# Experts' phase of an adaLN block with fast weights and mixture of experts: inner columns split 128 + 48, short down products of two tiles in the halves of the array

## What is computed

```python
B, S, D, E, F, FS = (4, 256, 256, 64, 176, 352)   # weights: w_gate, w_up (E, F, D), w_down (E, D, F)
...
buf = jnp.zeros((E, C, D), x.dtype).at[se, pos_c].add(jnp.where(valid[:, None], x[st], jnp.zeros((), x.dtype)))
g = jnp.einsum('ecd,efd->ecf', buf, w_gate)
u = jnp.einsum('ecd,efd->ecf', buf, w_up)
eo = jnp.einsum('ecf,edf->ecd', jax.nn.silu(g) * u, w_down)
```

## Time and profile before

| | us |
|---|---|
| median of 3 runs | 2373.19 (2371.55 to 2373.62) |
| profiled execution, its own time | 2371.46 |
| its span | 2369.4 |
| experts' phase in it (first gather issued to last copy-out) | about 1411.8 to 2060.5 |
| combine, behind it | to the end |

### The profile page before, as it was taken

The page is one execution under the profiler, slowest core; times in us unless marked ns, Lnnn a source line. Parts: engine busy times, 40 slices in busy tenths (PEclk is TensorE's granted clock), DMA queues, the critical chain, the costliest instruction groups (busy, mean ns, idle before and its releaser), DMA issues. The chain is left out here.

```text
span 2369.4 us, 41529 instructions
## 1 busy us (share of the span) xinstructions
PE 1772.2 (75%) x11445; PEld 1300.8 (55%) x11514; DVE 1265.8 (53%) x3323; ACT 939.5 (40%) x2156; POOL 899.2 (38%) x836
## 2 busy tenths in 40 slices
PE   3667638999999999846610539999999999875663
PEld 1444426777777777634500117777777777654542
DVE  2444426888888888635459972222222222245554
ACT  1232225777777777511101843333333333321110
POOL 1222312333333333345505014344433444257776
PEclk7666757999999999856655989999999999987776
DMA  2333341111111111045510016665556545444544
GB/s 69 101 113 97 93 125 24 42 42 42 42 42 42 42 42 42 23 116 145 148 40 0 1 33 180 185 180 170 166 166 171 170 134 105 107 119 140 149 136 124
DMA packets 269891, 231.43 MB, mean 98 GB/s; under 512 B 88624, under 2 KB 246672, under 8 KB 269728
## 3 DMA queue, kind: packets, MB, share of 16 engines
q1 hardware_dynamic: 211360, 136.99, 20.9%
q0 software_dynamic: 21504, 58.75, 9.9%
q10 hardware_dynamic: 36864, 33.57, 4.3%
HBM read 156.56 MB, written 72.65 MB: 97 GB/s over the span
## 5 line engine op out<-in xcount | busy, mean ns | idle before, releaser
L1698 POOL DMA_INDIRECT e_xg<-scratch_h,slots x256 | 255.6, 999 | 369.9 <-PE e_psX L1712 359.4
L1809 DVE COPY e_hT<-e_psH 88x256 f32<-88x256 f32 x256 | 107.7, 421 | 467.9 <-PE e_psH L1735 467.9
L1726 PE MATMUL e_psGU<-e_wgu,e_xT 128*128 x1024 | 349.5, 463 | 1.7 <-issue 0.9
L1742 PE MATMUL e_psD<-e_wd,e_hT 88*128 x1024 | 263.6, 379 | 0.0
L1075 POOL TENSOR_TENSOR f_wnr<-f_wss,f_half 128x4 f32<-128x4 f32 x96 | 111.1, 1157 | 390.5 <-DVE f_wss L1023 390.5
L1726 PEld LDWEIGHTS e_psGU<-e_wgu,e_xT 128*128 128x128 f32 x1024 | 192.0, 191 | 76.3 <-issue 6.9
L1930 POOL DMA_INDIRECT c_g<-scratch_eo,c_idx x192 | 196.3, 1023 | 76.0 <-issue 46.0
L1742 PEld LDWEIGHTS e_psD<-e_wd,e_hT 88*128 88x128 f32 x1024 | 173.8, 190 | 14.3 <-issue 0.3
L1787 ACT ACTIVATE e_eo<-e_psD 128x256 f32<-128x256 f32 x256 | 98.3, 384 | 179.2 <-PE e_psD L1742 179.2
L1777 ACT ACTIVATE e_sgm<-e_psGU 128x176 f32<-128x176 f32 x256 | 81.3, 318 | 212.3 <-PE e_psGU L1726 212.3
L354 PE MATMUL q_psQ<-q_wqkv,q_hT 128*128 128x512 f32 (+1 forms) x256 | 125.6, 649 | 31.6 <-DVE q_zl L430 29.8
(11 more groups left out here) (287 smaller groups left out, 4301.1 us busy)
## 6 DMA issues: line engine op xcount, KB each, us to landing
scratch_eo<-e_eo ACTq DMA_DIRECT2D x256, 128.0 KB, 1.8
scratch_qkvT<-q_tT SPq DMA_DIRECT2D x32, 384.0 KB, 2.8
e_wgu<-in_wgT SPq DMA_DIRECT2D x64, 176.0 KB
e_wgu<-in_wuT SPq DMA_DIRECT2D x64, 176.0 KB
e_wd<-in_wdT SPq DMA_DIRECT2D x64, 176.0 KB
scratch_kv<-q_y SPq DMA_DIRECT2D x32, 256.0 KB, 2.2
f_kvT<-scratch_qkvT SPq DMA_DIRECT2D x128, 64.0 KB
f_kv<-scratch_kv SPq DMA_DIRECT2D x64, 128.0 KB
```

Of the source, the lines that this page charges most:

```text
L1698: pool.indirect_dma_start(out=xg[n % GB][:, :], out_offset=None, in_=T["h2"], in_offset=bass.IndirectOffsetOnAxis(slots[:, n:n + 1], 0), b ...
L1726: mm = pe.matmul(psGU[:, j % 2, 0:2 * F], xT[:, j % 2, k, :], wgu[:, bass.ds(buf, 1), k, :].rearrange("p b n -> p (b n)"), start=(k == 0), ...
L1742: mm = pe.matmul(psD[:, j % 2, 0:D], hT[0:FH, j % 2, k, :], wd[0:FH, buf, k, :].rearrange("p b n -> p (b n)"), start=(k == 0), stop=(k == 1))
L1809: v.tensor_copy(hT[0:FH, b, :, :].rearrange("p k t -> p (k t)"), psH[0:FH, b, 0:2 * P]).then_inc(htd, 1)
```

## The change

The 176 inner columns are cut as 128 + 48 instead of 88 + 88.

- `hh` gets 64 columns of zeros between the two pieces. An even tile's short piece stands right behind its 128 columns, an odd tile's 64 columns further. The second transpose turns 48 columns for an even tile and 112 (the zeros and its own 48) for an odd one. So the 48 rows of the short piece come to stand at partition 0 or at partition 64.
- SyncE loads the down weights in three DMAs instead of one: 128 rows, and the last 48 rows twice, at partitions 0 and 64.
- VectorE copies the 48 rows of the tile's expert to a new buffer `wt`, for which it reads the expert from `need` and waits for `ready`. It makes two copies of `hT` (128 rows, 48 rows) instead of one and two products `hh` (128 columns, 48 columns) instead of one. `hT` is four tiles deep instead of two.
- TensorE does `down` for two tiles at once, in the step in which the odd one is due: the 128-row products of both, then the 48-row products of both, the even tile's on the partitions from 0, the odd tile's on those from 64. In the other step there is no `down`.

ScalarE's, POOL's and the other phases' programs are not touched.

```diff
@@ SyncE
-                sp.dma_start(wd[0:FH, bass.ds(buf, 1), :, :].rearrange("p b k n -> p (b k) n"), ...
-                sp.wait_ge(w_in, (ex + 1) * 48)
+                for rows, part, lo in ((P, 0, 0), (FT, 0, P), (FT, HP, P)):
+                    sp.dma_start(wd[part:part + rows, bass.ds(buf, 1), lo // P, :].rearrange("p b n -> p (b n)"),
+                                 T["wdT"][bass.ds(ex, 1), lo:lo + rows, :].rearrange("e p n -> (e p) n")).then_inc(w_in, 16)
+                sp.wait_ge(w_in, (ex + 1) * 80)
@@ TensorE (FT = 48, HP = 64)
             def turn_h(n, j):
+                part = HP * (n % 2)
                 pe.wait_ge(hd, thru(n))
                 pe.wait_ge(htd, thru(n - 2))
-                pe.transpose(psH[0:FH, j % 2, 0:P], hh[:, j % 2, 0:FH], ident[:, :])
-                pe.transpose(psH[0:FH, j % 2, P:2 * P], hh[:, j % 2, FH:F], ident[:, :]).then_inc(hp, 1)
...
+                pe.transpose(psH[:, j % 2, 0:P], hh[:, j % 2, 0:P], ident[:, :])
+                pe.transpose(psH[0:part + FT, j % 2, P:2 * P], hh[:, j % 2, P:P + part + FT], ident[:, :]).then_inc(hp, 1)
+
+            def down(n, experts):
+                for m in (n - 1, n):
+                    pe.wait_ge(htd, thru(m))
+                    pe.wait_ge(eod, thru(m - 2))
+                    pe.matmul(psD[:, m % 2, 0:D], hT[:, m % 4, 0, :],
+                              wd[:, bass.ds(experts[m % 2], 1), 0, :].rearrange("p b n -> p (b n)"), start=True, stop=False)
+                for m in (n - 1, n):
+                    part = HP * (m % 2)
+                    pe.matmul(psD[:, m % 2, 0:D], hT[part:part + FT, m % 4, 1, :], wt[part:part + FT, m // 2 % 2, :],
+                              start=False, stop=True).then_inc(dp, 1)
...
-                if real(n, 3):
-                    down(n - 3, (j - 3) % TI, out_of)
+                if real(n, 3) and (n - 3) % 2 == 1:
+                    down(n - 3, out_of)
@@ VectorE
+            v.memset(hh[:, 1, P:P + HP], 0.0).then_inc(blank, 1)
+            v.wait_ge(blank, 1)
...
                     v.wait_ge(hp, thru(m))
-                    v.wait_ge(dp, thru(m - 2))
-                    v.tensor_copy(hT[0:FH, b, :, :].rearrange("p k t -> p (k t)"), psH[0:FH, b, 0:2 * P]).then_inc(htd, 1)
+                    v.wait_ge(dp, thru(m - 4))
+                    part = HP * (m % 2)
+                    expert = v.value_load(need[0:1, m:m + 1], min_val=1, max_val=E)
+                    buf = bass.ds(v.snap((expert + (NB - 1)) % NB), 1)
+                    v.wait_ge(ready, expert)
+                    v.tensor_copy(wt[part:part + FT, m // 2 % 2, :], wd[part:part + FT, buf, 1, :].rearrange("p b n -> p (b n)"))
+                    v.tensor_copy(hT[:, m % 4, 0, :], psH[:, b, 0:P])
+                    v.tensor_copy(hT[part:part + FT, m % 4, 1, :], psH[part:part + FT, b, P:2 * P]).then_inc(htd, 1)
...
-                    v.tensor_tensor(hh[:, b, :], psGU[:, b, F:2 * F], sgm[:, b, :], ALU.mult).then_inc(hd, 1)
+                    part = P + HP * (n % 2)
+                    v.tensor_tensor(hh[:, b, 0:P], psGU[:, b, F:F + P], sgm[:, b, 0:P], ALU.mult)
+                    v.tensor_tensor(hh[:, b, part:part + FT], psGU[:, b, F + P:2 * F], sgm[:, b, P:F], ALU.mult).then_inc(hd, 1)
```

More of the change, by code:

```diff
@@ L1623, in phase_experts @@
     TI = 8
-    FH = F // 2
+    FT = F - P
+    HP = P // 2
     GB = 8
@@ L1641, in phase_experts @@
         sgm = sb("sgm", [P, 2, F])
-        hh = sb("hh", [P, 2, F])
-        hT = sb("hT", [P, 2, 2, P])
+        hh = sb("hh", [P, 2, P + HP + FT])
+        hT = sb("hT", [P, 4, 2, P])
+        wt = sb("wt", [P, 2, D])
         eo = sb("eo", [P, OB, D])
@@ L1655, in phase_experts @@
             "xp", "x", "gup", "sg", "h", "hp", "ht", "dp", "eo"))
+        blank = sems.take("e_blank")
         block = ctx.enter_context(nc.Block())
@@ L1681, in _ @@
                                  [bass.ds(ex, 1), :, :, :].rearrange("e p k n -> (e p) k n")).then_inc(w_in, 16)
-                sp.dma_start(wd[0:FH, bass.ds(buf, 1), :, :].rearrange("p b k n -> p (b k) n"),
-                             T["wdT"].rearrange("e (k p) n -> e p k n", p=FH)
-                             [bass.ds(ex, 1), :, :, :].rearrange("e p k n -> (e p) k n")).then_inc(w_in, 16)
-                sp.wait_ge(w_in, (ex + 1) * 48)
+                for rows, part, lo in ((P, 0, 0), (FT, 0, P), (FT, HP, P)):
+                    sp.dma_start(wd[part:part + rows, bass.ds(buf, 1), lo // P, :].rearrange("p b n -> p (b n)"),
+                                 T["wdT"][bass.ds(ex, 1), lo:lo + rows, :].rearrange("e p n -> (e p) n")).then_inc(w_in, 16)
+                sp.wait_ge(w_in, (ex + 1) * 80)
                 sp.sem_inc(ready, 1)
@@ L1731, in turn_h @@
             def turn_h(n, j):
+                part = HP * (n % 2)
                 pe.wait_ge(hd, thru(n))
                 pe.wait_ge(htd, thru(n - 2))
-                pe.transpose(psH[0:FH, j % 2, 0:P], hh[:, j % 2, 0:FH], ident[:, :])
-                pe.transpose(psH[0:FH, j % 2, P:2 * P], hh[:, j % 2, FH:F], ident[:, :]).then_inc(hp, 1)
[L1737 to L1744, removed]
+                pe.transpose(psH[:, j % 2, 0:P], hh[:, j % 2, 0:P], ident[:, :])
[10 more added lines that the diff above has]
+                              start=False, stop=True).then_inc(dp, 1)
+            out_of = {}
             def step(n, j):
@@ L1750, in step @@
                 if real(n, 3):
-                    out_of = expert_of(n - 3)
+                    out_of[(n - 3) % 2] = expert_of(n - 3)[1]
                 if real(n, 0):
```

## The result

| | before | changed |
|---|---|---|
| median, us | 2372.37 (2370.41 to 2373.62, 4 runs) | 2697.62 (2696.08 to 2700.33, 4 runs) |
| ratio | | 1.1373, 95% interval 1.1353 to 1.1393 |
| span of the profiled execution | 2369.4 | 2696.7 |
| mean granted clock over the span | 0.854 | 0.871 |

The change costs 325 us, 13.7%. I had forecast 2690 us, and the range was 2645 to 2765.

A forecast was written before the change was run, and what follows sets the result against it. The experts' phase was taken as bound by what TensorE streams. A pair of tiles was to go from 4.98 to 7.43 us, +314 over 128 pairs; with 2371.5 and 4 for small costs, 2690 us, range 2645 to 2765.

The forecast's parts named there:

- stall 1: TensorE after the short products: gate and up wait for ScalarE's late copy of x, 1.6 us a pair.
- stall 2: TensorE in the step without downs: gate and up wait for the copy of x after the turns, 0.7 us.
- What moves, and decides: the order of ScalarE: ScalarE stands at the even tile's copy-out, holding up silu and copy of x; gate and up 1.6 us late.
- The single step has lost its cover: In the step without downs, nothing fills TensorE's time during the copy of x; 0.7 us lost.
- VectorE's longer list: VectorE's register load (0.9 us) and five copies and products (1.15) delay TensorE's turn of the hidden tile about 0.25 us.
- The sum of TensorE alone: TensorE's streams per pair: 0.43 us gained by halves, 0.4 lost to four shape changes; 4.95 against 4.98.
- (a): Rival: TensorE's own sum decides, a pair 4.85 to 4.95 us, 2356 at best; chance 0.02.
- (b): Rival: the halves do not overlap or the 48-column turn spoils something; still 2690 us; no separate chance given.
- (c): Rival: VectorE becomes the bound, chain 2.9 us, a pair 8.2, total 2787; chance 0.1.
- (d): Rival: TensorE's clock falls in the stalls, a third of the pairs at about 11.5 us, total 2862; chance 0.08.
- The wait of `gate_up` for the copy of x: Sign in TensorE's waits: gate and up waiting for the copy of x, near 290 us in sum.
- The wait of the silu for TensorE: Sign in ScalarE's waits: the silu's wait for TensorE would be gone.

The follow-up runs named there:

- The second: The changed kernel with ScalarE's copy-outs of both tiles moved to the end of the step with the downs, behind silu and copy of x; 2518.93 us.
- the first experiment: The kernel before with only the downs of two tiles done together, hT four tiles deep, cut still 88 + 88; 2613.43 us.
- e6_same_half: As e5_wide_turn, but both tiles' short products lie on the partitions from 0, wt four deep; 2421.07 us, ratio 1.0201.
- e5_wide_turn: As e4_order_load_cover, but the second turn of an even tile also has 112 columns; 2368.45 us, ratio 0.9981.
- e4_order_load_cover: The changed kernel with copy-outs behind both downs, VectorE's early register load, x turned ahead of gate and up, copy of x before silu; 2363.21 us, ratio 0.996.
- e7_load: The changed kernel with only VectorE's register load and copy of short weights moved ahead of its wait for the turned tile; 2638.04 us.

## Why the prediction was right, point by point

**The pair.** The pieces from the short products of one pair to those of the next, as the prediction counted them and as the timeline has them. A `gate_up` behind a gap takes 1.28 instead of 1.19 to the next turn; these 0.09 are counted with the gap, since the prediction had put the exposed weight load there.

| piece | predicted | measured |
|---|---|---|
| short products to gate and up (stall 1 in it) | 2.06 | 2.02 + 0.09 = 2.11 |
| gate and up | 1.19 | 1.19 |
| turns of x to gate and up (stall 2 in it) | 1.14 | 1.06 + 0.09 = 1.15 |
| gate and up | 1.19 | 1.19 |
| turn of x to turn of `hh` (VectorE's chain in it) | 0.47 | 0.50 |
| turns of `hh` | 0.42 | 0.28 |
| 128-row downs | 0.96 | 1.04 |
| pair | 7.43 | 7.46 |

Two short-product rows of line 1749 119 pairs apart, near the start and near the end of the phase, confirm the pair: 1455.19 and 2343.02, or 7.46 each. (7.46 - 4.98) x 128 = 317 us, against 314 predicted. The other 8 of the 325 us lie outside the steady part, where I had put 4. The 7.6 us by which 2690 fell short are these two differences and 0.9 of the start (2372.37 for 2371.5), with rounding.

The other phases stand, as forecast: the first gather is at 1414.4 (1411.8 before, 2.6 us that come from phases the change does not touch) and the last copy-out ends at 2388.2 (2060.5 before), so the experts' phase is 325.1 us longer and ends 328 us later, for the 315 that I had said; behind it are 308.5 us, and 308.9 before.

**"What moves, and decides: the order of ScalarE": right.** The silu came 0.45 behind the copy-out (taken 0.48), the copy of x 0.22 behind it (0.22), the weight load 0.23 behind its end (0.24). The second and the first experiment show the cause, each from its side. One term was small: the copy-out starts 1703.71 - 1702.98 = 0.73 behind the first short record where I had 0.64, since the short records come late.

**"The single step has lost its cover": right.** Stall 2 was worked out at 0.70; it measures 1707.34 - 1706.72 + 0.09 = 0.71, and the reordering that puts a gate and up between gave back 0.78 per pair.

**"VectorE's longer list": right in its sum, by two errors that cancel.** From the turned tile to the copies it took 0.85 (taken 0.9), between TensorE's and SyncE's prices, nearer to TensorE's. The chain of five instructions took 1709.07 - 1707.73 = 1.34 instead of 1.15. The copy of weights takes 0.29 and not 0.42, but the three copies do not overlap: each starts 0.01 to 0.03 after the one before has ended, where I had let each begin 0.08 early by a row with another pair of instructions. TensorE's wait came out at 0.28 for 0.25; that the two errors cancel is luck.

The missing overlap has a cause that I had not seen, and the runs show it. It is missing only for the odd tile, whose short piece stands on the partitions from 64. For the even tile, all on the partitions from 0, the same three copies do begin 0.08 early:

```profile
1718.05 0.28 DVE L1823 COPY e_wt<-e_wd 48x256 f32 x1 [1.34 <-PE e_psH L1739]
1718.26 0.28 DVE L1824 COPY e_hT<-e_psH 128x128 f32<-128x128 f32 x1
1718.46 0.27 DVE L1825 COPY e_hT<-e_psH 48x128 f32<-48x128 f32 x1
```

In the steady part the second and the third copy begin 0.19 to 0.21 apart for every even tile and 0.30 to 0.31 for every odd one. In e6_same_half, where both tiles' pieces stand on the partitions from 0, they are 0.19 to 0.21 apart for both; this is one of its steps:

```profile
1702.87 0.29 DVE L1824 COPY e_hT<-e_psH 128x128 f32<-128x128 f32 x1 [2.40 <-PE e_psH L1739]
1703.08 0.27 DVE L1825 COPY e_hT<-e_psH 48x128 f32<-48x128 f32 x1
```

In e5_wide_turn, which differs from it in the place of the odd tile's piece and what follows from that, the odd tile's are 0.30 to 0.31 apart again. So a VectorE instruction behind one whose rows start at another partition begins only when that one has ended: 0.1 us at each of three places in the odd tile's list, or 1.34 us for the chain where it would be about 1.0. With 0.3 less, TensorE's wait of 0.28 would be gone or nearly so. That is an estimate from these rows, since no run has the changed kernel's order with both pieces at 0.

**"The sum of TensorE alone": right in its sum, wrong in its shares.** The gain of 0.43 is confirmed. I gave 0.2 us to the changes into and out of the half products and 0.2 to the 48-column turn. The first cost 0.37, since I had left out that the second record of the short group comes late as well, and the second cost nothing. So the pair on TensorE alone is 4.91 and not 4.95; that it is so near is luck in the shares. My range had a slip here too: three changes on the path at 0.2 instead of 0.1 give +38 us, as 0 gives -38, and not +25, which is what 0.16 gives. The result did not come near that bound.

The Trainium skill, TensorEngine Tiling (Array Packing), Key Properties, has it that a change of the tiling mode drains TensorE. The late records around the short products agree with that in kind: 0.37 us per pair. The 48-column turn, which would be a change as well if it ran in one of the modes with fewer columns that the page lists, shows no such price in the rows; no row shows in which mode it ran.

**The rivals.** (a) did not happen, but e4_order_load_cover is its case, made by hand: its pair is 4.91 where (a) had 4.85 to 4.95. (b) is out by the records. (c) is out: the pair is 7.46 and not 8.2, and VectorE's share in it is the 0.42 of e7_load. (d) is out by the granted clock of 1.00 in the window.

**What I had said the profile would show.** The wait of `gate_up` for the copy of x was to be near 290 us for 128 pairs. A 290 is there under another name, 289.8 us on the weight loads in 119 pairs, ended by "issue", but that it is the same number is luck. The weight loads' idle time begins while the records before still stream (1.72 us against 1.32 of TensorE's own in the row at 1705.00, 0.70 against 0.46 in the second stall), and my 290 was for 128 pairs and counted the way through the weight load. TensorE's own idle time ahead of `gate_up` is 155.1 us under "issue" and 56.1 under the copy of x, 211 us. The wait of the silu for TensorE was to be gone. It is not (174.4 us, 120 times): in the single step ScalarE is early, as the row at 1706.48 shows, and only in the double step it is the one that is late. I had drawn the double step's order and forgotten the other.

## What to carry to other kernels

Before work is moved to a later step, look in every engine's list for the instruction that waits for its result and ask what stands behind it: here a copy-out that nobody was in a hurry for held up two instructions that the producer itself needed, and cost more (179 us) than all the arithmetic of the change could gain (0.43 x 128 = 55). Work that is taken out of a step may have been the cover of another engine's latency; look for what else can stand there (here the next turns, ahead of the products). Count a product in a part of the array by its whole group, from the record before it to the record behind it: a gain of 0.43 us was worth 0.06. Count it on the copying engine too: the piece at partition 64 made each of VectorE's tiles that had one 0.3 us slower.

## What the runs showed of the hardware that was not expected

- The granted clock stayed full over 900 us in which TensorE stood 1.3 and 0.5 us in every 7.46 and was busy in 74%.
- A register load on VectorE with its register operations (0.30 + 0.19 us) stood in a stretch of 0.85 us from the end of the turn it waited for to the first copy.
- VectorE's instructions overlap by 0.08 us when their rows start at the same partition, and not when they start at 0 and 64 in turn (0.20 to 0.21 against 0.30 to 0.33 from start to start, e6_same_half against e5_wide_turn).
- The copy of 48 x 256 from SBUF to SBUF took 0.28 to 0.32 us most of the time, and 0.53 to 0.55 in 76 of 252 steps from 1435 to 2380, 72 of them double steps.

The Trainium skill, SBUF — State Buffer, Terms, says that VectorE and GpSimd share a pair of ports which one of them holds for a whole instruction, while the other is blocked. The long copies begin 0.53 to 0.56 us into one of POOL's gathers and end about 0.1 us behind it (1702.96 + 0.55 = 1703.51, the gather 1702.42 + 0.99 = 1703.41), which would fit. But the short one of the single step (1707.73 to 1708.02) lies wholly inside another gather, and so does one that begins at the same place as a long one (1627.90 to 1628.19, 0.54 us into the gather from 1627.36 to 1628.35), which would not. No run here takes the two apart, so this stays open. In the double step the long copy is off the path; in the four single steps that had one it is on it (the copy from 2340.07 took 0.54, and TensorE stood 0.73 us for `hh` at 2341.72).
